# Attention probabilities transposed in 32x32 blocks on VectorE and put in order through DRAM, in place of transposes on TensorE

## The chip, the cores and the metric

The kernel runs on one core of a Trainium2 chip, in one launch. The metric is the time of the execution on the device in microseconds, the median over the runs. Lower is better.

## The reference, cut to what matters

One layer of a graph transformer over 128 graphs of 128 nodes, width 384, eight heads of 48, all in float32:

```python
q = split_heads(x @ wq + bq); k = split_heads(x @ wk + bk); v = split_heads(x @ wv + bv)
scores = einsum('bhqd,bhkd->bhqk', q, k) * dh ** -0.5 + adj[:, None]
attn = softmax(scores, axis=-1)
ctx = einsum('bhij,bhjd->bhid', attn, v)
x1 = rmsnorm(x + ctx @ wo + bo, alpha1, gamma1)
x2 = rmsnorm(x1 + silu(x1 @ w1 + b1) @ w2 + b2, alpha2, gamma2)
out = layernorm(x + x2)
```

The change is about `attn`. The scores come out with the queries on the partitions and the keys along the row. The product with v contracts over the keys, so the keys have to lie on the partitions: every head of every graph needs its 128x128 probabilities transposed.

## The kernel before, in words

Two graphs make a group (`PAIR`); there are 64 groups, 256 tokens each. The matrix products of the layer's weights are made with each operand split in a high and a low part and three products each (`PASSES`), written `passes`, line 443. Weights stay in SBUF for the whole run.

The work is a pipeline over slots, written out by hand for each engine in its own `slot_program(t)`. In slot t the core does: the projections q, k, v of group t; the scores and softmax of group t-1; the context, output product and first norm of group t-2; the feed-forward (`up`, silu, `down`) of group t-3; and the last norm of group t-3 and t-4. There are 68 such slots, 0 to 67. Every engine works through its own list in order, and waits on semaphores where it needs another.

In one slot TensorE (PE) runs, in this order: context of both graphs (L495, L499), scores (L514), output product (L443, `wo_s`), q, k and v (L443), the 108 matmuls of `up` (L443, `w_s`; six pieces m = 0 to 5 of 18 matmuls), the transposes of the probabilities (L470, 16 of them), the transposes of the next group's x (L451 into `ps_work`, 6) and of x1 (L451 into `ps_att`, 6), and the 72 matmuls of `down` (L581).

The two PSUM tiles `ps_work` take turns. Piece m of `up` writes over what piece m-2 left, so it waits for ScalarE's silu of piece m-2:

```python
if m >= 2:
    pe.wait_ge(silu_ready[m - 2], through(g))
```

ScalarE (ACT) makes silu of a piece (L714) from PSUM into `h_raw`, which has two places; VectorE (DVE) then splits it into high and low (L883 and L885). Silu of piece m waits for `h_lo[m - 2]`, the split of piece m-2, because it writes over that place. The transposes of x also write `ps_work`, in two parts: four of them into the tile that piece 4 used, and then two into that of piece 5:

```python
for i, blocks in enumerate(((0, 1), (2,))):
    if live(g - LAG_FF - 1):
        pe.wait_ge(silu_ready[fc // 2 - 2 + i], through(g - LAG_FF - 1))
    ...
    transpose_rows(x_banks[i], x_in, blocks, xT_done[i])
```

Softmax: DVE adds the bias and takes the maximum (L823, L827), ACT takes the exponentials head by head (L660), DVE scales by the inverse sum (L833, L835; `normalise`, two halves of four heads for each graph). PE transposes the probabilities into `ps_att`, and ACT copies them back to `probs` (L649, `probsT_out`); the context of the next slot reads them as the moving operand.

The SP queue issues nearly all DMAs, in order: in a slot the residual x, the bias, the next x, `x_last`, ten small moves of q and k from `qk_flat` to `qk` (L359), the output of an earlier group (L363), and in slots 0 to 3 weights. In slot 3 six loads of w2 (L319) stand last on it; ACT (`weights_hi`, L634) and DVE (`weights_lo`, L802) split them between the silu pieces of that slot: two of them behind silu piece 2, two behind 3, two behind 4.

Of the kernel before, what the change touches and what calls it, by code (L numbers as in the profile page):

```python
# [14 lines left out]
HALF = 64  # L15
TILE = 32
HI, LO = 0, 1

# [8 lines left out]
def build_layer(nc, x, adj, wq, bq, wk, bk, wv, bv, wo, bo, w1, b1, w2, b2,  # L27
# [17 lines left out]
    with ctx:  # L45
# [108 lines left out]
        probsT_done = sems("probsT_done", PAIR)  # L154
        probsT_ready = sems("probsT_ready", PAIR)
        ctx_done = sems("ctx_done", PAIR)
        ctx_hi = sems("ctx_hi", PAIR)
# [43 lines left out]

        probs_words = probs[:].rearrange("p b h n -> p (b h n)")
        h_words = h_raw[:].rearrange("p a n -> p (a n)")
# [70 lines left out]
        def through(g, each=1):  # L274

            return (g + 1) * each

        x_banks = (ps_work[1][:, 0:2 * toks], ps_work[0][:, 0:toks])
        x1_banks = (ps_att[0][:, 0:2 * toks], ps_att[0][:, 2 * toks:3 * toks])
# [5 lines left out]
        def group_rows(ap, g):  # L285

            return ap[g * PAIR:(g + 1) * PAIR].rearrange("b n e -> n b e")

        block = ctx.enter_context(nc.Block())

        @block.sync
        def _(sp):
# [33 lines left out]
            def slot_program(t):  # L326
# [109 lines left out]
        def _(pe):  # L436
# [27 lines left out]
            def transpose_probs(g, b):  # L464
                pe.wait_ge(probs_ready[b], through(g, 2))
                if b == 0 and g == last:
                    for i in range(2):
                        pe.wait_ge(x1T_lo[i], through(g - 1))
                for head in range(HEADS):
                    mm = pe.transpose(ps_att[b][:, head * P:(head + 1) * P], probs[:, b, head, :], ident[:])  # L470
                mm.then_inc(probsT_done[b], 1)

            def transpose_x1(g):
                for b in range(PAIR):
                    pe.wait_ge(x1_ready[b], through(g))

                if g == last - 1:
                    pe.wait_ge(scores_biased[0], through(last))
                else:
                    pe.wait_ge(probsT_ready[0], through(min(g + 1, last)))  # L480
                for i, blocks in enumerate(((0, 1), (2,))):
                    transpose_rows(x1_banks[i], x1[:, g % 2], blocks, x1T_done[i])

            def context(g, b):
                pe.wait_ge(probsT_ready[b], through(g))
                pe.wait_ge(v_ready[b], through(g))
# [5 lines left out]
                for side in range(2):  # L492
                    for pair in range(hp):
                        head = 2 * pair + side
                        pe.matmul(ps_work[b][pair * TILE:(pair + 1) * TILE, 2 * P:3 * P], v_rest[:, g % 2, b, head, :],  # L495
                                  probs[:, b, place(head), :], start=(side == 0), stop=(side == 1))
                for head in range(HEADS):
                    p0, at = head % 4 * TILE, head // 4 * P
                    mm = pe.matmul(ps_work[b][p0:p0 + TILE, at:at + P], v_first[:, g % 2, b, head, :],  # L499
                                   probs[:, b, place(head), :], start=True, stop=True)  # L500
                mm.then_inc(ctx_done[b], 1)

            def scores(g, b):
                if b == 0:
                    pe.wait_ge(qk_moved, through(g, 16 * len(moves)))
                if live(g - 1):
                    pe.wait_ge(probsT_ready[b], through(g - 1))
                if b == 0 and live(g + LAG_SCORES - LAG_FF):
# [76 lines left out]
            def slot_program(t):  # L585
# [43 lines left out]
        def _(act):  # L629
# [17 lines left out]
            def probsT_out(g, b):  # L647
                act.wait_ge(probsT_done[b], through(g))
                act.activation(probs[:, b].rearrange("p h n -> p (h n)"), ps_att[b][:],  # L649
                               ACT.Copy).then_inc(probsT_ready[b], 1)  # L650

# [5 lines left out]
            def exponentials(g, b):  # L657
                act.wait_ge(max_ready[b], through(g))
                for head in range(HEADS):
                    e = act.activation(probs[:, b, head, :], probs[:, b, head, :], ACT.Exp,  # L660
                                       bias=neg_max[:, b, head:head + 1], accum_out=row_sum[:, b, head:head + 1])
# [58 lines left out]
            def slot_program(t):  # L720
# [69 lines left out]
        def _(dve):  # L790
# [27 lines left out]
            def bias_and_max(g, b):  # L818
                dve.wait_ge(scores_done[b], through(g))
                if b == 0:  # L820

                    dve.wait_ge(bias_loaded, through(g, 16))
                dve.tensor_tensor(probs[:, b], ps_att[b][:].rearrange("p (h n) -> p h n", n=P),  # L823
                                  bias[:, b, :].unsqueeze(1).to_broadcast([P, HEADS, P]),
                                  ALU.add).then_inc(scores_biased[b], 1)
                dve.wait_ge(scores_biased[b], through(g))
                dve.tensor_reduce(neg_max[:, b, :], probs[:, b], AX.X, ALU.max,  # L827
                                  negate=True).then_inc(max_ready[b], 1)

            def normalise(g, b, half):  # L830
# [3 lines left out]
                dve.wait_ge(inv_ready[b], through(g, 2) - 1 + half)  # L834
                dve.tensor_tensor(probs[:, b, heads], probs[:, b, heads],  # L835
                                  row_inv[:, b, heads].unsqueeze(2).to_broadcast([P, hp, P]),
                                  ALU.mult).then_inc(probs_ready[b], 1)

            def keys_out(g):
# [76 lines left out]
            def slot_program(t):  # L916
# [93 lines left out]
```

## Time and profile before

| | us |
|---|---|
| median of three runs | 2911.36 (2911.35 to 2911.66) |
| the profiled execution | 2910.08 |
| its span in the trace | 2908.3 |
| TensorE busy | 2882.5 (99%) |
| VectorE busy | 1846.2 (63%) |
| ScalarE busy | 1431.3 (49%) |
| GpSimd busy | 684.3 (24%) |
| DMA, mean rate | 59 GB/s |

The profiled execution is 1.8 us longer than its span, for what lies around the first and the last record. A matmul's row in the timeline begins where it starts and has its modelled end behind the start of the next, so the cost of a run of matmuls is read from one row's start to the start of the next row. "PEld" is the load of the stationary operand, which runs beside the matmuls. `[us <-X]` at the end of a row is the idle time of that engine just before it and who ended it.

### The profile page before, as it was taken

To read this page: it belongs to the slowest core of one execution; us is meant where nothing else is said; L and a number is where in the kernel's file an instruction comes from. 1 tells how busy PE (TensorE), PEld (TensorE's weight loads), DVE (VectorE), ACT (ScalarE), POOL (GpSimd) and SP (SyncE) were. 2 spreads that over 40 slices of the span, in tenths; PEclk is the share of its full clock that TensorE was granted. 3 is DMA by queue.
4 is the path that set the end of the run, shared out by engine and by line. 5 is a ranking of instruction groups with operands and counts; after the bars stand their busy time and mean duration, and the time that the engine had idled before them with its cause. 6 is when DMAs were issued, how large, how long until landed. Compare 5 with 4: busy or idle time off the path is not lost.

```text
span 2908.3 us, 62626 instructions
## 1 busy us (share of the span) xinstructions
PE 2882.5 (99%) x25216; PEld 2841.8 (98%) x25216; DVE 1846.2 (63%) x3621; ACT 1431.3 (49%) x4259; POOL 684.3 (24%) x968
## 2 busy tenths in 40 slices
PE   7999999999999999999999999999999999999998
PEld 7999999999999999999999999999999999999998
DVE  6766666656666566566665666666656666566564
ACT  5544545445445454454544544545445445454452
POOL 0222222221222222212222222222221222222222
PEclk9999999999999999999999999999999999999999
DMA  5211212112112121121221211212112112121110
GB/s 172 76 54 57 65 43 68 56 50 64 54 57 65 41 70 52 53 65 48 63 59 47 66 54 56 64 43 68 56 49 64 54 57 65 41 70 53 52 47 28
DMA packets 155490, 171.93 MB, mean 59 GB/s; under 512 B 18624, under 2 KB 155200, under 8 KB 155200
## 3 DMA queue, kind: packets, MB, share of 16 engines
q1 hardware_dynamic: 151952, 166.92, 19.7%
q8 instruction: 200, 3.28, 0.5%
q10 hardware_dynamic: 3248, 0.99, 0.2%
q14 instruction: 90, 0.74, 0.1%
HBM read 92.35 MB, written 25.17 MB: 40 GB/s over the span
## 4 chain that ended last, share of the span: by engine, by line
PE 97%; DVE 1%; DMA 1%; SPq 1%; ACT 0%; issue 0%; POOL 0%; ACTq 0%; POOLq 0%; DVEq 0%
PE ps_work L443 48%; PE ps_rows L581 27%; PE ps_rows L443 7%; PE ps_att L514 4%; PE ps_att L470 4%; PE ps_work L495 2%; PE ps_work L499 2%; PE ps_att L451 1%; PE ps_work L451 1%; SPq L359 0%; DMA x_in<-in_x 0%; DVE w_s L802 0%; DMA stage<-in_L_gnn_wq 0%; POOL x_in L413 0%; DVE neg_max L827 0%
## 5 line engine op out<-in xcount | busy, mean ns | idle before, releaser
L443 PE MATMUL ps_work<-x1T,w_s 128*128 128x256 f32 x6912 | 821.9, 280 | 1.8 <-ACT h_raw L714 1.8
L443 PEld LDWEIGHTS ps_work<-x1T,w_s 128*128 128x128 f32 x6912 | 819.3, 188 | 2.2 <-ACT h_raw L714 2.2
L581 PE MATMUL ps_rows<-w_s,h 128*128 128x384 f32 x4608 | 815.0, 337 | 0.0
L581 PEld LDWEIGHTS ps_rows<-w_s,h 128*128 128x128 f32 x4608 | 796.2, 188 | 0.0
L714 ACT ACTIVATE h_raw<-ps_work,b_col 128x256 f32<-128x256 f32 x768 | 322.3, 471 | 533.1 <-PE ps_work L443 524.9
L660 ACT ACTIVATE probs<-probs,neg_max 128x128 f32<-128x128 f32 x1024 | 396.4, 391 | 190.3 <-DVE neg_max L827 190.3
L425 POOL TENSOR_TENSOR x<-x,rows 128x768 f32<-128x768 f32 x64 | 117.5, 1836 | 1160.8 <-DVE h L885 1160.8
L689 ACT ACTIVATE squares<-y 128x384 f32<-128x384 f32 x128 | 67.1, 524 | 627.8 <-DVE y L894 627.8
L883 DVE CAST h<-h_raw 128x512 fp32r<-128x512 f32 x384 | 163.8, 427 | 249.0 <-ACT h_raw L714 248.8
L894 DVE TENSOR_TENSOR y<-ps_rows,x 128x384 f32<-128x384 f32 x128 | 71.4, 558 | 385.0 <-PE ps_rows L581 385.0
L885 DVE TENSOR_TENSOR h<-h_raw,h 128x512 fp32r<-128x512 f32 x384 | 265.9, 692 | 13.2
L391 POOL TENSOR_SCALAR mean_sq<-sum_sq 128x1 f32<-128x1 f32 x256 | 53.8, 210 | 816.8 <-ACT squares L678 467.0
L443 PE MATMUL ps_work<-xT,wq_s 128*128 128x256 f32 x1728 | 216.0, 282 | 2.9 <-DVE xT L809 2.9
L443 PE MATMUL ps_rows<-wo_s,ctxT 128*128 128x384 f32 x1152 | 218.1, 343 | 0.5 <-DVE ctxT L814 0.5
L443 PEld LDWEIGHTS ps_work<-xT,wq_s 128*128 128x128 f32 x1728 | 213.6, 190 | 3.5 <-DVE xT L809 3.3
L443 PE MATMUL ps_work<-xT,wk_s 128*128 128x256 f32 x1728 | 213.2, 280 | 0.0
L443 PE MATMUL ps_work<-wv_s,xT 128*128 128x384 f32 x1152 | 211.4, 337 | 1.0 <-DVE qk_flat L845 0.5
L443 PEld LDWEIGHTS ps_work<-xT,wk_s 128*128 128x128 f32 x1728 | 207.4, 188 | 0.0
L443 PEld LDWEIGHTS ps_rows<-wo_s,ctxT 128*128 128x128 f32 x1152 | 197.6, 188 | 8.4 <-issue 0.7
L443 PEld LDWEIGHTS ps_work<-wv_s,xT 128*128 128x128 f32 x1152 | 197.6, 188 | 1.8 <-DVE qk_flat L845 1.1
L660 ACT ACTIVATION_READ_ACCUMULATOR probs<-probs,neg_max 128x1 f32 x1024 | 193.4, 189 | 0.0
L835 DVE TENSOR_TENSOR probs<-probs,row_inv 128x512 f32<-128x512 f32 x256 | 177.9, 695 | 8.7
(75 smaller groups left out, 3439.2 us busy)
## 6 DMA issues: line engine op xcount, KB each, us to landing
x_in<-in_x SPq DMA_DIRECT2D x128, 384.0 KB, 3.2
qk<-qk_flat SPq DMA_DIRECT2D x381, 96.0 KB, 2.3
x_last<-in_x SPq DMA_DIRECT2D x64, 384.0 KB, 3.7
out<-y SPq DMA_DIRECT2D x63, 384.0 KB, 2.7
bias<-in_adj SPq DMA_DIRECT2D x64, 128.0 KB, 2.1
qk<-qk_flat SPq DMA_DIRECT2D x127, 64.0 KB, 2.0
qk<-qk_flat SPq DMA_DIRECT2D x127, 32.0 KB, 2.0
stage<-in_L_gnn_w SPq DMA_DIRECT2D x17, 192.0 KB, 4.0
```

The lines of the kernel that those rows point to most:

```text
L425: pool.tensor_tensor(x1[:, g_ff % 2], x1[:, g_ff % 2], row(B2), ALU.add).then_inc(x1_b2_ready, 1)
L443: mm = pe.matmul(ps_out, stationary(sta), moving(mov), start=(i == 0), stop=(i == n - 1))
L470: mm = pe.transpose(ps_att[b][:, head * P:(head + 1) * P], probs[:, b, head, :], ident[:])
L514: mm = pe.matmul(ps_att[b][:, at:at + P], qk[p0:p0 + dh, Q, c, b * P:(b + 1) * P], qk[p0:p0 + dh, K, c, b * P:(b + 1) * P], start=True, st ...
L581: mm = pe.matmul(ps_rows[b][:, 0:d], h[:, sta, m, b * P:(b + 1) * P], w2_s[:, mov, m, :], start=(m == 0 and i == 0), stop=(m == fc - 1 and ...
L660: e = act.activation(probs[:, b, head, :], probs[:, b, head, :], ACT.Exp, bias=neg_max[:, b, head:head + 1], accum_out=row_sum[:, b, head: ...
L689: act.activation(squares[:], y[:, b, :], ACT.Square, accum_out=sum_sq2[:, b:b + 1]).then_inc(sq2_ready[b], 1)
L714: e = act.activation(h_raw[:, m % 2, j * toks:(j + 1) * toks], ps_work[(m + 1) % 2][:, j * toks:(j + 1) * toks], ACT.Silu, bias=b1_col[:, ...
L835: dve.tensor_tensor(probs[:, b, heads], probs[:, b, heads], row_inv[:, b, heads].unsqueeze(2).to_broadcast([P, hp, P]), ALU.mult).then_inc ...
L883: dve.tensor_copy(hi, h_raw[:, m % 2, :]).then_inc(h_hi[m], 1)
L885: dve.tensor_tensor(h[:, LO, 2 * m:2 * m + 2, :].rearrange("p c n -> p (c n)"), h_raw[:, m % 2, :], hi.bitcast(F32), ALU.subtract).then_in ...
L894: dve.tensor_tensor(y[:, b, :], ps_rows[b][:, 0:d], x1[:, g % 2, b, :], ALU.add).then_inc(res2_ready[b], 1)
```

## The change

The groups 0, 1 and 63 go on as before. For the other 61 (g = 2 to 62), PE's 16 transposes and ACT's two copies are gone. DVE transposes the 128x1024 probabilities of a graph in place, in 32x32 blocks, in one instruction. That leaves block (i, j) in its old place with its inside transposed; the blocks still have to change places. SP stores the whole tile to a DRAM buffer and loads it again, with block (i, j) going to (j, i): one store of 512 KB and four loads of 128 KB for each graph, in runs of 1 KB. For such groups the probabilities are laid out with the key block j outside and the head inside (`by_head`), so that a run of all eight heads is 1 KB long. The steps that read or write `probs` in these groups (L823, L827, L835, L660 and the context's matmuls) see a head as four pieces of 32 numbers, 256 apart.

The waits follow: `context` waits for the four loads (`blocks_loaded`) in place of ACT's copy; `scores` and `transpose_x1` wait for `scores_biased` of the group before, in place of ACT's copy, since nothing but the scores now uses `ps_att` there.

The diff, cut to its core:

```diff
-        probs = sb("probs", [P, PAIR, HEADS, P])
+        probs = sb("probs", [P, PAIR, HEADS * P])
...
+        def by_head(g, b):
+            order = "p (h j r) -> p h j r" if blocks_by_pe(g) else "p (j h r) -> p h j r"
+            return probs[:, b].rearrange(order, h=HEADS, r=TILE)
...
+        def by_dma(g):
+            return min(g, last - 1) - 1
...
+        def blocks_by_pe(g):
+            return g < 2 or g == last
+        probs_dram = nc.dram_tensor("probs_blocks", (PAIR, P, QUARTERS, HEADS * TILE), F32, kind="Internal").ap()
...
+            def move_blocks(g):
+                for b in range(PAIR):
+                    sp.wait_ge(blocks_ready[b], by_dma(g))
+                    if by_dma(g) > 1:
+                        sp.wait_ge(blocks_loaded[b], 16 * QUARTERS * (by_dma(g) - 1))
+                    sp.dma_start(probs_dram[b], probs[:, b].rearrange("p (j c) -> p j c", j=QUARTERS)).then_inc(
+                        blocks_stored[b], 16)
+                for b in range(PAIR):
+                    sp.wait_ge(blocks_stored[b], 16 * by_dma(g))
+                    for j in range(QUARTERS):
+                        sp.dma_start(probs[j * TILE:(j + 1) * TILE, b].rearrange("p (i c) -> p i c", i=QUARTERS),
+                                     probs_dram[b, :, j].rearrange("(i r) c -> r i c", r=TILE)).then_inc(
+                                         blocks_loaded[b], 16)
...
+                if live(t - LAG_SCORES) and not blocks_by_pe(t - LAG_SCORES):
+                    move_blocks(t - LAG_SCORES)
                 for n in loads_due.get((t, 1), ()) if t > 0 else ():
                     load_weights(n)
...
             def context(g, b):
-                pe.wait_ge(probsT_ready[b], through(g))
+                if blocks_by_pe(g):
+                    pe.wait_ge(probsT_ready[b], by_pe(g))
+                else:
+                    pe.wait_ge(blocks_loaded[b], 16 * QUARTERS * by_dma(g))
...
-                                  probs[:, b, place(head), :], start=(side == 0), stop=(side == 1))
+                                  by_head(g, b)[:, place(head)], start=(side == 0), stop=(side == 1))
...
-                if live(g_scores) and g_scores < last:
+                if live(g_scores) and g_scores < last and blocks_by_pe(g_scores):
                     for b in range(PAIR):
                         transpose_probs(g_scores, b)
...
-                if live(g_scores) and g_scores < last:
+                if live(g_scores) and g_scores < last and blocks_by_pe(g_scores):
                     for b in range(PAIR):
                         probsT_out(g_scores, b)
...
+            def transpose_blocks(g, b):
+                dve.wait_ge(probs_ready[b], through(g, 2))
+                dve.transpose(probs[:, b], probs[:, b]).then_inc(blocks_ready[b], 1)
...
                 if live(t):
                     values_out(t, 1)
+                if live(g_scores) and not blocks_by_pe(g_scores):
+                    transpose_blocks(g_scores, 0)
                 if live(g_out):
                     layer_norm(g_out, 1)
...
                     for half in range(2):
                         normalise(g_scores, 1, half)
+                    if not blocks_by_pe(g_scores):
+                        transpose_blocks(g_scores, 1)
                 if live(g_ff):
                     for m in range(fc // 2):
                         split_h(g_ff, m)
```

What that makes of the order of instructions. On PE, from `up` to `down` of a slot in the middle, before:

```order
L443 MATMUL ps_work<-x1T,w_s 128x256 x108
L470 MATMUL ps_att<-ident,probs 128x128 x16
L451 MATMUL ps_work<-ident,x_in 128x128 x6
L451 MATMUL ps_att<-ident,x 128x128 x6
L581 MATMUL ps_rows<-w_s,h 128x384 x72
L495 MATMUL ps_work<-probs,v_rest 32x128 x8
```

and now:

```order
L482 MATMUL ps_work<-x1T,w_s 128x256 x108
L490 MATMUL ps_work<-ident,x_in 128x128 x6
L490 MATMUL ps_att<-ident,x 128x128 x6
L627 MATMUL ps_rows<-w_s,h 128x384 x72
L539 MATMUL ps_work<-probs,v_rest 32x128 x8
```

The transposes of the probabilities no longer stand between `up` and the transposes of x.

On DVE, in the same slot, from the end of `values_out` to the first split of silu's output, before:

```order
L859 TENSOR_TENSOR v_rest<-ps_work,rows 128x4x16 x2
L913 TENSOR_SCALAR y<-y,mean_var,inv_std 128x384
L873 SCALAR_TENSOR_TENSOR x<-x,inv_rms,rows 128x384
L877 TENSOR_TENSOR x<-x,rows 128x384
L833 RECIPROCAL row_inv<-row_sum 128x4
L835 TENSOR_TENSOR probs<-probs,row_inv 128x512
L833 RECIPROCAL row_inv<-row_sum 128x4
L835 TENSOR_TENSOR probs<-probs,row_inv 128x512
L883 CAST h<-h_raw 128x512
L885 TENSOR_TENSOR h<-h_raw,h 128x512
```

and now:

```order
L910 TENSOR_TENSOR v_rest<-ps_work,rows 128x4x16 x2
L888 STREAM_TRANSPOSE probs<-probs 128x1024
L964 TENSOR_SCALAR y<-y,mean_var,inv_std 128x384
L924 SCALAR_TENSOR_TENSOR x<-x,inv_rms,rows 128x384
L928 TENSOR_TENSOR x<-x,rows 128x384
L879 RECIPROCAL row_inv<-row_sum 128x4
L881 TENSOR_TENSOR probs<-probs,row_inv 128x4x4x32
L879 RECIPROCAL row_inv<-row_sum 128x4
L881 TENSOR_TENSOR probs<-probs,row_inv 128x4x4x32
L888 STREAM_TRANSPOSE probs<-probs 128x1024
L934 CAST h<-h_raw 128x512
L936 TENSOR_TENSOR h<-h_raw,h 128x512
```

Two `STREAM_TRANSPOSE` of 128x1024 stand ahead of the first split (CAST and TENSOR_TENSOR of `h`), and the scaling by the inverse sum has its rows in pieces of 32.

On the SP queue, from the last move of q and k (48x2x256) to the next load of x, before:

```order
L359 DMA qk<-qk_flat 48x2x256 x2
L363 DMA out<-y 128x2x384
L310 DMA x_in<-in_x 128x2x384
L341 DMA bias<-in_adj 128x2x128
L300 DMA x_in<-in_x 128x2x384
```

and now:

```order
L396 DMA qk<-qk_flat 48x2x256 x2
L400 DMA out<-y 128x2x384
L349 DMA probs_blocks<-probs 128x1024 x2
L354 DMA probs<-probs_blocks 32x4x256 x8
L333 DMA x_in<-in_x 128x2x384
L378 DMA bias<-in_adj 128x2x128
L323 DMA x_in<-in_x 128x2x384
```

Two stores and eight loads stand between the output and the load of the residual; in slot 3 they stand ahead of the six loads of w2.

## Rows read from the trace of the kernel before

**Rows 1.** Page: the chain that ended last, by engine.

```profile
PE 97%; DVE 1%; DMA 1%; SPq 1%; ACT 0%; issue 0%; POOL 0%; ACTq 0%; POOLq 0%; DVEq 0%
```

**Rows 2.** Waits of TensorE from 180 to 2800 us (us, times, longest).

```profile
PE ps_att L451 <- ACT probs L649: 0.3, 1, 0.3
```

**Rows 3.** Timeline, PE, one slot: start, us, engine, line, out<-in.

```profile
1504.06 0.65 PE L495 MATMUL ps_work<-probs,v_rest 128*32 128x128 f32 x16
...
1505.94 2.06 PE L514 MATMUL ps_att<-qk 48*128 48x128 f32 x32
...
1520.64 12.83 PE L443 MATMUL ps_work<-x1T,w_s 128*128 128x256 f32 x108
...
1533.32 1.91 PE L470 MATMUL ps_att<-ident,probs 128*128 128x128 f32 x16
1535.06 0.82 PE L451 MATMUL ps_work<-ident,x_in 128*128 128x128 f32 x6
...
1536.29 8.92 PE L581 MATMUL ps_rows<-w_s,h 128*128 128x384 f32 x50
...
1548.95 0.65 PE L495 MATMUL ps_work<-probs,v_rest 128*32 128x128 f32 x16
```

**Rows 4.** Timeline, ACT, same slot.

```profile
1522.95 0.84 ACT L714 ACTIVATE h_raw<-ps_work,b_col 128x256 f32<-128x256 f32 x2 [2.14 <-PE ps_work L443]
...
1533.51 0.84 ACT L714 ACTIVATE h_raw<-ps_work,b_col 128x256 f32<-128x256 f32 x2 [1.27 <-PE ps_work L443]
```

**Rows 5.** Timeline, DVE, same slot.

```profile
1525.04 0.70 DVE L885 TENSOR_TENSOR h<-h_raw,h 128x512 fp32r<-128x512 f32 x1
```

**Rows 6.** Groups by form, whole run: xcount, busy us, mean ns.

```profile
L827 DVE TENSOR_REDUCE neg_max<-probs 128x8 f32<-128x1024 f32 x128 | 156.2, 1220 | 4.4
L883 DVE CAST h<-h_raw 128x512 fp32r<-128x512 f32 x384 | 163.8, 427 | 249.0 <-ACT h_raw L714 248.8
L857 DVE TENSOR_TENSOR v_first<-ps_work,rows 128x256 f32<-128x256 f32 x128 | 53.9, 421 | 4.3 <-PE ps_work L443 2.2
```

**Rows 7.** Timeline around 2822 us, slot 64: who released silu and TensorE.

```profile
2821.99 0.69 DVE L885 TENSOR_TENSOR h<-h_raw,h 128x512 fp32r<-128x512 f32 x1
2822.78 0.84 ACT L714 ACTIVATE h_raw<-ps_work,b_col 128x256 f32<-128x256 f32 x2 [4.04 <-DVE h L885]
2823.67 4.50 PE L443 MATMUL ps_work<-x1T,w_s 128*128 128x256 f32 x36 [1.07 <-ACT h_raw L714]
```

**Rows 8.** Timeline, SP queue, same slot as rows 3.

```profile
1518.68 6.98 SPq L359 DMA_DIRECT2D qk<-qk_flat  x10
1525.76 0.54 SPq L363 DMA_DIRECT2D out<-y  x1
1535.95 0.37 SPq L310 DMA_DIRECT2D x_in<-in_x  x1
```

**Rows 9.** Page, DMA issues: KB each, median us to landing.

```profile
out<-y SPq DMA_DIRECT2D x63, 384.0 KB, 2.7
bias<-in_adj SPq DMA_DIRECT2D x64, 128.0 KB, 2.1
stage<-in_L_gnn_w SPq DMA_DIRECT2D x17, 192.0 KB, 4.0
```

**Rows 10.** Timeline, slot 3: up, the six w2 loads, the copies and silu of piece 3.

```profile
84.06 12.83 PE L443 MATMUL ps_work<-x1T,w_s 128*128 128x256 f32 x108
...
88.85 2.99 SPq L319 DMA_DIRECT2D stage<-in_L_gnn_w  x6
...
91.57 1.02 ACT L634 ACTIVATE w_s<-stage 128x384 fp32r<-128x384 f32 x2
92.70 0.84 ACT L714 ACTIVATE h_raw<-ps_work,b_col 128x256 f32<-128x256 f32 x2
```

**Rows 11.** Timeline: TensorE after an early gap; and its clock there (third from the right).

```profile
24.81 2.77 PE L514 MATMUL ps_att<-qk 48*128 48x128 f32 x32 [3.19 <-DMA qk<-qk_flat]
24.80:27.50 2.70, 2.69 (x32) 2.48 (x32) 1.64 (x3) 0.89 (x3) 0.00 (x0) 0.71 0.66 230
```

More of the change, by code:

```diff
@@ L16 @@
 TILE = 32
+QUARTERS = P // TILE
 HI, LO = 0, 1
@@ L155, in build_layer @@
         probsT_ready = sems("probsT_ready", PAIR)
+        blocks_ready = sems("blocks_ready", PAIR)
+        blocks_stored = sems("blocks_stored", PAIR)
+        blocks_loaded = sems("blocks_loaded", PAIR)
         ctx_done = sems("ctx_done", PAIR)
@@ L200, in staged_at @@
             return n if n < places else (n - places) % STAGE_SLOTS
-        probs_words = probs[:].rearrange("p b h n -> p (b h n)")
+        probs_words = probs[:].rearrange("p b n -> p (b n)")
         h_words = h_raw[:].rearrange("p a n -> p (a n)")
@@ L276, in through, with by_pe @@
             return (g + 1) * each
+        def by_head(g, b):
+            order = "p (h j r) -> p h j r" if blocks_by_pe(g) else "p (j h r) -> p h j r"
+            return probs[:, b].rearrange(order, h=HEADS, r=TILE)
+        def by_pe(g):
+            return g + 1 if g < 2 else 3 if g == last else 2
+        def by_dma(g):
+            return min(g, last - 1) - 1
         x_banks = (ps_work[1][:, 0:2 * toks], ps_work[0][:, 0:toks])
@@ L469, in transpose_probs @@
                 for head in range(HEADS):
-                    mm = pe.transpose(ps_att[b][:, head * P:(head + 1) * P], probs[:, b, head, :], ident[:])
+                    mm = pe.transpose(ps_att[b][:, head * P:(head + 1) * P], probs[:, b, head * P:(head + 1) * P], ident[:])
                 mm.then_inc(probsT_done[b], 1)
@@ L475, in transpose_x1 @@
                     pe.wait_ge(x1_ready[b], through(g))
-                if g == last - 1:
-                    pe.wait_ge(scores_biased[0], through(last))
+                if g + 1 > last:
+                    pe.wait_ge(probsT_ready[0], by_pe(last))
+                elif g + 1 < last and blocks_by_pe(g + 1):
+                    pe.wait_ge(probsT_ready[0], by_pe(g + 1))
                 else:
-                    pe.wait_ge(probsT_ready[0], through(min(g + 1, last)))
+                    pe.wait_ge(scores_biased[0], through(g + 1))
                 for i, blocks in enumerate(((0, 1), (2,))):
@@ L499, in context @@
                     mm = pe.matmul(ps_work[b][p0:p0 + TILE, at:at + P], v_first[:, g % 2, b, head, :],
-                                   probs[:, b, place(head), :], start=True, stop=True)
+                                   by_head(g, b)[:, place(head)], start=True, stop=True)
                 mm.then_inc(ctx_done[b], 1)
@@ L505, in scores @@
                     pe.wait_ge(qk_moved, through(g, 16 * len(moves)))
-                if live(g - 1):
-                    pe.wait_ge(probsT_ready[b], through(g - 1))
+                if live(g - 1) and blocks_by_pe(g - 1):
+                    pe.wait_ge(probsT_ready[b], by_pe(g - 1))
+                elif live(g - 1):
+                    pe.wait_ge(scores_biased[b], through(g - 1))
                 if b == 0 and live(g + LAG_SCORES - LAG_FF):
@@ L647, in probsT_out @@
             def probsT_out(g, b):
-                act.wait_ge(probsT_done[b], through(g))
-                act.activation(probs[:, b].rearrange("p h n -> p (h n)"), ps_att[b][:],
-                               ACT.Copy).then_inc(probsT_ready[b], 1)
+                act.wait_ge(probsT_done[b], by_pe(g))
+                act.activation(probs[:, b], ps_att[b][:], ACT.Copy).then_inc(probsT_ready[b], 1)
             def context_hi(g, b):
@@ L659, in exponentials @@
                 for head in range(HEADS):
-                    e = act.activation(probs[:, b, head, :], probs[:, b, head, :], ACT.Exp,
+                    e = act.activation(by_head(g, b)[:, head], by_head(g, b)[:, head], ACT.Exp,
                                        bias=neg_max[:, b, head:head + 1], accum_out=row_sum[:, b, head:head + 1])
@@ L822, in bias_and_max @@
                     dve.wait_ge(bias_loaded, through(g, 16))
-                dve.tensor_tensor(probs[:, b], ps_att[b][:].rearrange("p (h n) -> p h n", n=P),
-                                  bias[:, b, :].unsqueeze(1).to_broadcast([P, HEADS, P]),
+                dve.tensor_tensor(by_head(g, b), ps_att[b][:].rearrange("p (h j r) -> p h j r", j=QUARTERS, r=TILE),
+                                  bias[:, b, :].rearrange("p (j r) -> p j r", r=TILE).unsqueeze(1).to_broadcast(
+                                      [P, HEADS, QUARTERS, TILE]),
                                   ALU.add).then_inc(scores_biased[b], 1)
                 dve.wait_ge(scores_biased[b], through(g))
-                dve.tensor_reduce(neg_max[:, b, :], probs[:, b], AX.X, ALU.max,
+                dve.tensor_reduce(neg_max[:, b, :], by_head(g, b), AX.XY, ALU.max,
                                   negate=True).then_inc(max_ready[b], 1)
@@ L834, in normalise @@
                 dve.wait_ge(inv_ready[b], through(g, 2) - 1 + half)
-                dve.tensor_tensor(probs[:, b, heads], probs[:, b, heads],
-                                  row_inv[:, b, heads].unsqueeze(2).to_broadcast([P, hp, P]),
+                dve.tensor_tensor(by_head(g, b)[:, heads], by_head(g, b)[:, heads],
+                                  row_inv[:, b, heads].unsqueeze(2).unsqueeze(3).to_broadcast(
+                                      [P, hp, QUARTERS, TILE]),
                                   ALU.mult).then_inc(probs_ready[b], 1)
+            def transpose_blocks(g, b):
+                dve.wait_ge(probs_ready[b], through(g, 2))
+                dve.transpose(probs[:, b], probs[:, b]).then_inc(blocks_ready[b], 1)
             def keys_out(g):
```

## The prediction

> **What bounds the kernel now.** I read the chain of waits first. TensorE holds 97% of it [rows 1]. Then its waits: from 180 to 2800 us TensorE waited once, for 0.3 us [rows 2]. So every matmul taken off this engine shortens the kernel, unless a wait opens in its place. The other engines matter only through what TensorE waits for, and TensorE waits for none of them because each is in time; the question is by how much. That is read inside one slot, since all slots from 3 to 62 run alike: from one context to the next is 1548.95 - 1504.06 = 44.89 us [rows 3].
>
> The 16 transposes of the probabilities start at 1533.32 and those of x at 1535.06 [rows 3]: 1.74 us a slot, 0.109 us each.
>
> **What the removed transposes cover.** The transposes of x begin with four that need silu piece 4 and go on with two that need silu piece 5. That silu runs from 1533.51 to 1534.35 [rows 4], and `up` ends just before 1533.32. Now the probabilities' transposes fill this time. Without them the first four start at 1533.32 and are done at 1533.32 + 4 x 0.109 = 1533.76. The other two wait for 1534.35 plus the step from silu to TensorE. In slot 64 that step can be seen: silu ends at 2822.78 + 0.84 = 2823.62, TensorE starts at 2823.67 [rows 7], 0.05 us; I take 0.08, hence 1534.43. New stall: 0.67 us. A slot gains 1.74 - 0.67 = 1.07 us, if nothing else comes late.
>
> **What VectorE gets.** Two transposes of 128x1024 in place stand ahead of the first split of silu's output. No row shows this operation. The nearest in size is the maximum over 128x1024 at 1.22 us [rows 6]. Below it, two CASTs of 128x512 at 0.427 give 0.85 us, for an operation that reads and writes faster. Above it, two passes over the tile give 2.44 us. I take 1.22, since the maximum too goes over 1024 elements once. The Trainium skill, Vector Engine (DVE) Microarchitecture Reference, section 3.8, says that the transpose is pipelined to sustain one element per cycle in each lane; nothing in this trace shows it, and the sum by it would be the one below.
>
> The first split now ends at 1525.04 + 0.70 = 1525.74 [rows 5]. It moves by 2 x 1.22 = 2.44 to 1528.18. Silu piece 2 writes over what it reads. The step from a split to silu is seen in slot 64: the split ends at 2822.68, silu starts at 2822.78 [rows 7], 0.10 us. So silu 2 starts at 1528.28, ends 0.84 later, and TensorE can begin piece 4 at 1529.17. A piece of `up` takes (1533.32 - 1520.64) / 6 = 2.11 us, so piece 4 is due at 1520.64 + 4 x 2.11 = 1529.09 [rows 3]. The stall is 0.08; I take 0.1. In general it is the shift less 2.36 us: **the free room is almost exactly used up**. Piece 5 needs silu 3, which needs the second split, at 1528.18 + 1.2 = 1529.4; silu 3 would be done near 1530.4 and piece 5 is due at 1531.2, so nothing more is lost. Net gain of a slot: 1.07 - 0.1 = **0.97 us**.
>
> **Edits taken at nothing.** DVE's bias, maximum and scaling work in pieces of 32. `v_first` is already written in pieces of 32: 256 elements at 421 ns [rows 6], against 1024 at 1220. The difference is 799 ns for 768 elements, one rate for both shapes. The exponentials on ACT are in pieces too; ACT is idle 2.14 us before silu piece 0 [rows 4]. Without that cover, each 0.1 us of lateness in silu would cost up to 6 us over 60 slots. The context's matmuls read pieces of 32 as the moving operand. They take from 1504.06 to 1505.94 [rows 3], 1.9 us a slot; I take no change since the columns are as many, and the bounds are 0 and that time again. ACT's two copies vanish; nothing waited for them but the transposes of x1, in slot 63. `scores` waits for `scores_biased`, a slot old.
>
> **The way through DRAM.** SP issues the output until 1525.76 + 0.54 = 1526.30 [rows 8], then store 0. Store 1 needs DVE's second transpose, near 1527.1. A 384 KB output lands in 2.7 us and 192 KB of weights in 4.0 [rows 9]; for 512 KB I take 3, bounds 2.1 and 5.3. Store 0 has landed at 1529.3. Eight loads at 0.55 an issue (between 0.37 and 0.70 [rows 8]) are out by 1533.7 and landed 2.1 us later (128 KB, bias [rows 9]), at 1535.8. The context that needs them is due at about 1548. That is 12 us of room, on a path that takes ten, so nothing is lost. The residual x behind them on SP goes out at 1535.95 now [rows 8], later than 1533.7, so it isn't held up.
>
> **Slot 3, once.** The six w2 loads now stand behind this traffic. Before, they were issued from 88.85; the copies of the first two began at 91.57, silu 3 at 92.70 [rows 10]. After: store 0 at 88.85, landed 91.9, eight issues at 0.55 until 96.3; the first w2 load is 7.5 us late. ACT stands in its copies until 91.57 + 7.5 = 99.1. Silu 3 starts at 100.2 and ends at 101.1, where piece 5 is due at 84.06 + 5 x 2.11 = 94.6: TensorE idles 6.5 us. Silu 4 and 5 each follow two copies, 1.95 us apiece, so silu 5 ends at 105.0. Eight transposes later `down` starts at 105.9. It was due 15.65 us after `up` (as in rows 3) less 0.97, at 98.7: 7.2 us lost. After an early gap of 3.19 us the granted clock was 0.71 for 2.7 us [rows 11], between the levels of 1.2 and 2.4 GHz, 0.8 us of work lost. I add 0.8 for that: **8 us**, bounds 5 and 12.
>
> **Slot 63** has no transposes of x. It gains 1.74 and the one wait of 0.3 behind ACT's copy [rows 2], less 0.1: 2.0 us.
>
> **Sum.** 60 x 0.97 = 58.2, plus 2.0, less 8 = 52.2 us. The profiled execution took 2910.08 us, its span 2908.3. 2910.1 - 52.2 = 2857.9. The median of the runs lies 1.3 above the profiled execution: **2859 us**. A measurement of this kernel can tell about 0.2%, 6 us, from no change.
>
> **Rivals.**
> 1. *The transpose on VectorE is slow.* At two passes, 2.44 us each, the shift is 4.88 and piece 4 stalls 4.88 - 2.36 = 2.52 us. A slot loses 2.52 - 1.07 = 1.45 us. With slot 63 (loses 0.45) and slot 3 (8) the time is 2911.4 + 87 + 8.5 = **3007 us**, slower. It decides from 1.66 us a transpose: there the stall is 0.96 and the gains are gone. For it: 4-byte elements move across lanes, and no row shows the rate. Against: every float32 operation of DVE in this trace runs at least at the rate of the maximum. Chance 0.12. Between 1.5 and 1.66 us the time is 2892 to 2911; with other small losses the stretch from 2885 to 2905 gets 0.08.
> 2. *The context's matmuls slow down with pieces of 32.* Doubled, they cost 1.9 us in each of 61 slots: 2859 + 116 = 2975 us. Every other moving operand here is contiguous, so the trace is silent. 0.03.
> 3. *The blocks come late.* Every us beyond the 12 of room costs 60 us; at 14 us more than I take, 2859 + 120 = 2979. It would need landings over three times those of [rows 9]. The Trainium skill, VectorE: DVE Perf Modes, "The three transpose paths", warns that a plain DMA that transposes by strides can be 19 times slower than the hardware's transposing DMA when the destination's innermost stride is large; here that stride is one element and the runs are 1 KB. 0.02.
> 4. *The cover isn't needed*: the transposes of x don't stall, and no `up` piece does. 60 x 1.74 + 2 - 8 = 98 us, **2813 us**. The silu row speaks against it: it ends 0.6 us after the four transposes would. 0.04.
> 5. *Nothing to measure*, the stall near break-even or the gain lost elsewhere: 2911, 0.03.
>
> The same page of the Trainium skill, "Rules for kernel authors", says to transpose 128x128 on TensorE if PSUM will do as destination. It speaks against the change and would give rival 1's sign. The rows say otherwise here: the engine it favours is the one in the chain, and VectorE has room for all but 0.1 us.
>
> **Chances.** The forecast, 2848 to 2885, has 0.68. With the stretch above it (0.08) and rival 4 (0.04) faster has 0.80; same 0.03; slower 0.12 + 0.03 + 0.02 = 0.17. The low end of the range is no stall in `up` (6 us), a slot 3 of 5 us, and a piece of rival 4: 2842. The high end takes in transposes up to 1.6 us: 2908.
>
> **What would show it.** Right: no L470 rows in the middle, slots of 43.9 us, TensorE waiting for silu once at the x transposes for about 0.67 us in 60 slots, and for 0.1 or less in `up`; `STREAM_TRANSPOSE` at 1.2 to 1.3 us; a gap of 6 to 7 us in slot 3; the eight loads landed 10 us ahead of the context. Wrong: a transpose of over 1.6 us, context rows longer than before, or TensorE waiting for `probs` from a DMA.

## The result and the profile after

| | before | after |
|---|---|---|
| median of the runs, us | 2911.5 | 2863.14 (2862.74 to 2863.66, 4 runs) |
| the profiled execution, us | 2910.08 | 2862.81 |
| its span, us | 2908.3 | 2861.0 |

The ratio is 0.9833, with a 95% interval of 0.9821 to 0.9845: 48 us or 1.7% less, where 52 were forecast (2859 us). From the page after, the span, the busy shares and the chain by engine:

```profile
span 2861.0 us, 61404 instructions
...
PE 2799.9 (98%) x24240; PEld 2742.2 (96%) x24240; DVE 1968.0 (69%) x3743; ACT 1326.6 (46%) x4137; POOL 686.1 (24%) x968
...
PE 94%; ACT 2%; DVE 1%; SPq 1%; DMA 1%; issue 0%; POOL 0%; ACTq 0%; POOLq 0%; DVEq 0%
```

TensorE's share of the chain fell from 97% [rows 1] to 94%, and ACT has 2% in it: silu now releases TensorE in every slot. The groups by form (count | busy us, mean ns) give the one price that no row of before had, the last line; the two above it are the steps that now work in pieces of 32:

```profile
L881 DVE TENSOR_TENSOR probs<-probs,row_inv 128x512 f32<-128x512 f32 x256 | 177.9, 695 | 8.7
L873 DVE TENSOR_REDUCE neg_max<-probs 128x8 f32<-128x1024 f32 x128 | 156.2, 1221 | 4.4
...
L888 DVE STREAM_TRANSPOSE probs<-probs 128x1024 f32<-128x1024 f32 x122 | 151.3, 1240 | 2.1
```

The transpose takes 1.24 us for 128x1024, where 1.22 was taken. The maximum in pieces of 32 is at 1221 ns against 1220 [rows 6].

One slot in the timeline, PE, ACT, DVE and SP together, answering to [rows 3, 4, 5, 8]:

```profile
1484.59 0.65 PE L539 MATMUL ps_work<-probs,v_rest 128*32 128x128 f32 x16
...
1501.18 12.94 PE L482 MATMUL ps_work<-x1T,w_s 128*128 128x256 f32 x108
...
1501.98 1.24 DVE L888 STREAM_TRANSPOSE probs<-probs 128x1024 f32<-128x1024 f32 x1
...
1506.36 1.25 DVE L888 STREAM_TRANSPOSE probs<-probs 128x1024 f32<-128x1024 f32 x1
...
1507.95 0.69 DVE L936 TENSOR_TENSOR h<-h_raw,h 128x512 fp32r<-128x512 f32 x1
...
1508.73 0.84 ACT L759 ACTIVATE h_raw<-ps_work,b_col 128x256 f32<-128x256 f32 x2 [2.29 <-DVE h L936]
...
1510.38 3.67 SPq L354 DMA_DIRECT2D probs<-probs_blocks  x8
...
1513.96 0.60 PE L490 MATMUL ps_work<-ident,x_in 128*128 128x128 f32 x4
1514.16 0.84 ACT L759 ACTIVATE h_raw<-ps_work,b_col 128x256 f32<-128x256 f32 x2 [1.28 <-PE ps_work L482]
...
1515.05 0.44 PE L490 MATMUL ps_work<-ident,x_in 128*128 128x128 f32 x2 [0.49 <-ACT h_raw L759]
...
1515.90 12.74 PE L627 MATMUL ps_rows<-w_s,h 128*128 128x384 f32 x72
...
1528.57 0.64 PE L539 MATMUL ps_work<-probs,v_rest 128*32 128x128 f32 x16
```

The next context starts at 1528.57, so a slot is 43.98 us, 0.91 less than the 44.89 of before. `up` runs from 1501.18 to 1513.96, 12.78 us against 12.68: its first split ends at 1508.64, silu piece 2 waits for it and starts at 1508.73. Then four transposes of x start at 1513.96, the two others at 1515.05, behind the silu of 1514.16. From the end of `up` to `down` it is 1.94 us against 2.97 [rows 3]. So a slot gained 1.03 and lost 0.10. The only wait of TensorE that the list of waits has between 180 and 2750 us (us, times, longest):

```profile
PE ps_work L490 <- ACT h_raw L759: 28.6, 58, 0.5
```

The "0.5" is the idle time behind the modelled end of the four transposes; from start to start the row costs 1.09 - 0.44 = 0.65 us.

Slot 3 answers to [rows 10]. The SP queue (two stores, eight loads, then the six w2 loads), then ACT's copies of w2 and TensorE's last piece of `up`, then the window of that piece with TensorE's granted clock third from the right:

```profile
90.78 1.82 SPq L349 DMA_DIRECT2D probs_blocks<-probs  x2
93.76 3.67 SPq L354 DMA_DIRECT2D probs<-probs_blocks  x8
97.47 2.80 SPq L342 DMA_DIRECT2D stage<-in_L_gnn_w  x6
```

```profile
100.88 1.05 ACT L680 ACTIVATE w_s<-stage 128x384 fp32r<-128x384 f32 x2 [6.67 <-DMA stage<-in_L_gnn_w]
...
102.71 4.21 PE L482 MATMUL ps_work<-x1T,w_s 128*128 128x256 f32 x18 [5.99 <-ACT h_raw L759]
```

```profile
102.70:106.70 4.00, 3.99 (x18) 4.00 (x19) 3.93 (x8) 2.33 (x6) 0.00 (x0) 0.50 0.01 2
```

```profile
86.00 10.72 PE L482 MATMUL ps_work<-x1T,w_s 128*128 128x256 f32 x90
...
108.70 12.74 PE L627 MATMUL ps_rows<-w_s,h 128*128 128x384 f32 x72
121.37 0.65 PE L539 MATMUL ps_work<-probs,v_rest 128*32 128x128 f32 x16
```

The w2 loads went out at 97.47 where they had gone out at 88.85; 1.94 us of that is that the slot's `up` itself starts later, at 86.00 where it was 84.06 [rows 10]. ACT waited 6.67 us for them, TensorE 5.99, and then made 18 matmuls at a granted clock of 0.50, which is 1.2 GHz, in 4.0 us in place of 2.1.

The whole difference of the spans can be laid out from the starts of the contexts. Up to the context of slot 4, which began at 112.37 before, the kernel is 121.37 - 112.37 = 9.0 us later. From there to the context of slot 63, 59 slots, it takes 2594.52 us where 2648.70 were taken: 54.2 less. Slot 63 takes 42.60 in place of 44.76: 2.2 less. The rest is alike within 0.1 us. 54.2 + 2.2 - 9.0 = 47.4, against 2908.3 - 2861.0 = 47.3.

The 9.0 us are of two kinds. From the start of `up` in slot 3 to the context of slot 4 it takes 35.37 us where 28.31 were taken, 7.06 more. The other 1.94 were lost ahead of that `up`, and 1.16 of them by 15.07 us (`wk_s` started at 13.91 before), long before any group goes the new way. They don't come from the change: in the eleven traces of this document, the first kernel's among them, TensorE has the same work up to that point, and this `up` starts anywhere between 83.2 and 87.4 us (at 87.3 in experiment 7, which has nothing of the new way). Why the start-up differs so stays open. So a difference of a few us between two medians can be start-up, and the mean time of a slot is given with them below. It is the time from the context of slot 4 to that of slot 63, divided by 59: 44.89 us before and 43.98 after.

### The profile page after: what moved, and what is told of

Its sections match the earlier page's. It is cut to its first block, busy times and chain, and to the rows that moved or that the text cites. A ratio compares the mean times of both kernels' runs of the same rounds, so it can differ in the third digit from the quotient of the medians.

```text
span 2861.0 us, 61404 instructions
## 1 busy us (share of the span) xinstructions
PE 2799.9 (98%) x24240; PEld 2742.2 (96%) x24240; DVE 1968.0 (69%) x3743; ACT 1326.6 (46%) x4137; POOL 686.1 (24%) x968
## 4 chain that ended last, share of the span: by engine, by line
PE 94%; ACT 2%; DVE 1%; SPq 1%; DMA 1%; issue 0%; POOL 0%; ACTq 0%; POOLq 0%; DVEq 0%
PE ps_work L482 48%; PE ps_rows L627 28%; PE ps_rows L482 7%; PE ps_att L560 4%; PE ps_work L539 2%; PE ps_work L543 2%; ACT h_raw L759 2%; PE ps_att L490 1%; PE ps_work L490 1%; SPq L396 1%; DMA x_in<-in_x 0%; DVE w_s L847 0%; DMA stage<-in_L_gnn_wq 0%; POOL x_in L452 0%; DVE neg_max L873 0%
## 5 line engine op out<-in xcount | busy, mean ns | idle before, releaser
L482 PE MATMUL ps_work<-x1T,w_s 128*128 128x256 f32 x6912 | 830.7, 281 | 7.8 <-ACT h_raw L759 7.8
```

The source lines that it names most:

```text
L482: mm = pe.matmul(ps_out, stationary(sta), moving(mov), start=(i == 0), stop=(i == n - 1))
```

## The experiments

The theory to be tested: the change frees 1.74 us of TensorE a slot, and three waits of TensorE give some of it back, each with its own cause. They are silu piece 5 ahead of the last transposes of x (0.65 us), silu piece 2 behind the late split (0.1 us), and the w2 loads of slot 3 (8 to 9 us, once). The rival of each is that the loss comes from something shared (DMA traffic, memory, ACT) and would only move. Every edit is on the kernel after the change unless it says otherwise.

**1. The w2 loads first.**

```diff
+                for n in loads_due.get((t, 1), ()) if t > 0 else ():
+                    load_weights(n)
                 if live(t - LAG_SCORES) and not blocks_by_pe(t - LAG_SCORES):
                     move_blocks(t - LAG_SCORES)
-                for n in loads_due.get((t, 1), ()) if t > 0 else ():
-                    load_weights(n)
```

> The six w2 loads of slot 3 go to the SP queue ahead of the stores and loads of the blocks. My theory: the 6 us gap of TensorE before up piece 5 of slot 3 and the 4.2 us piece at a granted clock of 0.50 behind it come from these loads alone; both go, and slot 3 gets about 8.5 us back: 2863.1 - 8.5 = 2854.6 us. Rival: ACT is late in slot 3 because VectorE's two transposes delay the splits, and the loads are only seen waiting; then the time stays within 2 us of 2863.

Measured 2853.96 us (2853.73 to 2855.89), 9.2 less. Neither the gap nor the slow piece is left in slot 3: `up` takes 12.68 us there. The rival is out.

```profile
84.08 12.83 PE L482 MATMUL ps_work<-x1T,w_s 128*128 128x256 f32 x108
...
111.36 0.64 PE L539 MATMUL ps_work<-probs,v_rest 128*32 128x128 f32 x16
```

From `up` to the next context it is 27.28 us in place of 35.37: the loads cost 8.1 us. The rest isn't theirs: this trace starts `up` 1.92 us earlier, and its later slots take 1.0 us more in all (8.1 + 1.9 - 1.0 = 9.0, the difference of the two spans).

**2. The transposes of x1 between those of x.**

```diff
                 for i, blocks in enumerate(((0, 1), (2,))):
+                    if i == 1 and between is not None:
+                        transpose_x1(between)
...
-                    transpose_x(t + 1)
-                if live(g_attn):
+                    transpose_x(t + 1, g_attn)
+                elif live(g_attn):
                     transpose_x1(g_attn)
```

> The six transposes of x1, which wait for nothing late, go between the four and the two transposes of x. My theory: the wait of 0.65 us before the last two transposes of x is pure lateness of silu piece 5, so six other transposes of 0.65 us fill it, in 60 slots: 60 x 0.65 = 39 us less, 2824 us, and the wait row all but vanishes. Rival: the wait only moves, to the first matmuls of down or to the next slot's context, because silu 5 and the splits behind it set the pace there too: 2850 to 2863 us.

Measured 2824.51 us (2821.91 to 2826.16), 38.6 less; a ratio to the kernel before of 0.9705 [0.9691, 0.972]. The timeline of TensorE at the end of a slot's `up`:

```profile
1534.29 0.60 PE L490 MATMUL ps_work<-ident,x_in 128*128 128x128 f32 x4
1534.73 0.82 PE L490 MATMUL ps_att<-ident,x 128*128 128x128 f32 x6
1535.39 0.44 PE L490 MATMUL ps_work<-ident,x_in 128*128 128x128 f32 x2
1535.58 12.74 PE L629 MATMUL ps_rows<-w_s,h 128*128 128x384 f32 x72
```

All twelve transposes and the start of `down` follow without a wait: 1.29 us in place of 1.94. The time didn't move elsewhere: the mean slot is 43.34 us, 0.64 less.

**3. The second transpose behind the first split.**

```diff
                         normalise(g_scores, 1, half)
-                    if not blocks_by_pe(g_scores):
-                        transpose_blocks(g_scores, 1)
...
                         split_h(g_ff, m)
                         weights_lo(t, m)
+                        if m == 0 and live(g_scores) and not blocks_by_pe(g_scores):
+                            transpose_blocks(g_scores, 1)
```

> VectorE's transpose of the second graph goes behind the first split of silu's output in place of ahead of it. My theory: up takes 12.78 us a slot in place of 12.68 because the first split is late; with the split 1.2 us earlier silu piece 2 is in time and 60 x 0.1 = 6 us are gained: 2857 us. Rival: the 0.1 us comes from traffic (the DMAs now at 105 GB/s, or VectorE and TensorE reading the same memory), and moving the instruction changes nothing: 2863 us.

Measured 2857.71 us (2856.94 to 2858.85), 5.4 less. `up` is back at 12.67 us a slot and the mean slot at 43.86 us, 0.115 less, or 6.8 us over 59 slots; up to slot 4 this trace is 2.8 us later, half of it ahead of `up` in slot 3. The 0.1 us was the late split.

**4. Three transposes of the second graph in place of one.**

```diff
                 dve.wait_ge(probs_ready[b], through(g, 2))
+                if b == 1:
+                    for i in range(2):
+                        dve.transpose(probs[:, b], probs[:, b]).then_inc(blocks_again, 1)
+                        dve.wait_ge(blocks_again, 2 * (by_dma(g) - 1) + i + 1)
```

> VectorE transposes the second graph's tile three times in place (two more of 1.25 us, one after the other). My theory: the room of 2.36 us is used up, so each further us on VectorE ahead of the first split is a us of the slot: 61 x 2.5 = 153 us more, about 3016 us, and slower than the kernel before. Rival: VectorE's lateness is partly absorbed (by the later pieces of up, or by the wait before the transposes of x, which would shrink as up gets longer): under 2960 us.

Measured 3093.20 us (3092.74 to 3093.72), 230 more: 3.77 us a slot for 2.5 us of VectorE. The direction is right, the size isn't. One slot, then the windows behind the gap (clock third from the right):

```profile
1531.17 2.52 DVE L891 STREAM_TRANSPOSE probs<-probs 128x1024 f32<-128x1024 f32 x2
...
1536.11 0.84 ACT L760 ACTIVATE h_raw<-ps_work,b_col 128x256 f32<-128x256 f32 x2 [4.85 <-DVE h L941]
...
1537.00 5.83 PE L483 MATMUL ps_work<-x1T,w_s 128*128 128x256 f32 x36 [2.40 <-ACT h_raw L760]
...
1542.67 0.60 PE L491 MATMUL ps_work<-ident,x_in 128*128 128x128 f32 x4
```

```profile
1537.00:1539.00 2.00, 2.00 (x9) 2.00 (x10) 1.93 (x5) 0.84 (x2) 0.00 (x0) 0.50 0.76 231
1539.00:1541.00 2.00, 2.00 (x15) 2.00 (x14) 0.21 (x1) 0.27 (x1) 0.00 (x0) 0.77 1.00 236
1541.00:1542.60 1.60, 1.60 (x16) 1.60 (x15) 0.97 (x2) 0.57 (x2) 0.00 (x0) 1.00 0.46 98
```

Piece 4 of `up` was due at 1525.99 + 4 x 2.11 = 1534.44 and starts at 1537.00, 2.56 us late. The two pieces left then take 1542.67 - 1537.00 = 5.67 us, where 4.23 is their time at full clock: 1.44 us more. The granted clock is 0.50 for the first 2 us and 0.77 for the next 2. So this wait is paid one and a half times. With the 0.10 us that `up` was late already, 2.56 + 1.44 - 0.10 = 3.90 us, and the slot shown takes 47.86 us, 3.88 more.

**5. A shorter gap.** The same place, with two transposes of half the tile ahead of the one.

```diff
+                        dve.transpose(probs[:, b, 0:4 * P], probs[:, b, 0:4 * P]).then_inc(blocks_again, 1)
```

> Ahead of its transpose of the second graph VectorE transposes the first half of the tile (128x512) twice in place: 2 x 0.71 plus two steps, about 1.47 us more, where the kernel with three whole transposes had 2.5 us more and TensorE idle 2.40 us a slot, with a granted clock of 0.50 for 2 us behind each gap. Theory A, the clock answers to any such wait in up: the gap of about 1.4 us costs about 1.3 us of slow matmuls more, 61 x 2.8 = 170 us, about 3033 us. Theory B, the gap of 1.4 us leaves the clock at full speed, as the one of 0.49 us does: 61 x 1.47 = 90 us, about 2953 us.

Measured 2954.70 us (2953.29 to 2955.63), 91.6 more: 1.50 us a slot for 1.47 of VectorE. Theory B holds. The piece behind the gap, and its window:

```profile
1514.13 4.49 PE L483 MATMUL ps_work<-x1T,w_s 128*128 128x256 f32 x36 [1.33 <-ACT h_raw L760]
```

```profile
1514.10:1516.10 2.00, 1.97 (x16) 1.97 (x17) 1.93 (x5) 0.84 (x2) 0.00 (x0) 1.00 0.72 229
```

TensorE is idle 1.33 us and its clock stays at 1.00. In this `up` a gap of 1.33 us costs itself, one of 2.40 us costs 1.4 us more.

**6. Twice through DRAM**, on top of experiment 1.

```diff
+                for b in range(PAIR):
+                    sp.wait_ge(blocks_loaded[b], 16 * QUARTERS * by_dma(g))
...
+                    sp.dma_start(again_dram[b], probs[:, b].rearrange("p (j c) -> p j c", j=QUARTERS)).then_inc(
+                        again_stored[b], 16)
...
+                        sp.dma_start(probs[rows_j, b].rearrange("p (i c) -> p i c", i=QUARTERS),
+                                     again_dram[b, rows_j]).then_inc(again_loaded[b], 16)
```

> On top of the w2 loads ahead of the blocks (2854.0 us): every block goes to DRAM and back a second time, in the same order, before the context may read it. Traffic of the blocks doubles and the path from the first store to the last landing grows from about 10 to about 20 us. My theory: it had 11 to 12 us of room, so the time stays within 3 us of 2854. Rival: the way through DRAM is already nearly at its limit, or its traffic slows matmuls and other transfers: at least 10 us more, 2864 us or beyond.

Measured 2854.69 us (2852.41 to 2855.58), 0.7 more than experiment 1, within its spread, and the mean slot is 43.97 us against 43.99 there. SP's second trip in a slot, and the context behind it:

```profile
1501.95 3.69 SPq L357 DMA_DIRECT2D probs<-probs_blocks  x8
1506.42 2.53 SPq L364 DMA_DIRECT2D probs_again<-probs  x2
1509.68 4.34 SPq L370 DMA_DIRECT2D probs<-probs_again  x8
```

```profile
1520.08 0.65 PE L554 MATMUL ps_work<-probs,v_rest 128*32 128x128 f32 x16
```

The last load is issued by 1514.02 and, at a median landing of 2.9 us, is there near 1517; the context starts at 1520.08. Even two trips fit, with 3 us left. The mean rate of the DMAs rises from 105 to 150 GB/s, and nothing on TensorE slows.

**7. No transposition at all.**

```diff
-                    pe.wait_ge(blocks_loaded[b], 16 * QUARTERS * by_dma(g))
+                    pe.wait_ge(probs_ready[b], through(g, 2))
...
-                if live(t - LAG_SCORES) and not blocks_by_pe(t - LAG_SCORES):
-                    move_blocks(t - LAG_SCORES)
...
-                    transpose_blocks(g_scores, 0)
...
-                        transpose_blocks(g_scores, 1)
```

> Leaves out the transposition of the probabilities of groups 2 to 62 altogether: no transposes on VectorE, no stores and loads; the context reads the untransposed probabilities. My theory: what VectorE and the DMAs cost here is the 0.1 us a slot of up (6 us) and slot 3 (9 us), so 2848 us; the wait of 0.65 us ahead of the transposes of x stays, since it comes from silu. Rival: the block traffic costs more than its waits show (contention in SBUF or with other DMAs): under 2843 us.

This kernel leaves the transposition out, so what it returns is not the layer's output; only its time is of use. Measured 2847.88 us (2845.38 to 2849.11), 15.3 less: the 9.2 of experiment 1 and the 5.4 of experiment 3 make 14.6. Its mean slot is 43.86 us, the same as in experiment 3, which transposes. The new way of transposing costs nothing beyond the two waits already named. The wait ahead of the transposes of x is there as before.

**8. All three repairs,** the diffs of experiments 1 to 3 together.

> The w2 loads ahead of the blocks, the transposes of x1 between those of x, and VectorE's second transpose behind the first split, together. My theory: the three losses are separate waits of TensorE and add up: 2863.1 - 9.2 - 38.6 - 5.4 = 2810 us. Rival: with one gone another takes its place (down behind the splits, or ACT behind the later transposes of x): over 2818 us.

Measured 2808.20 us (2807.36 to 2809.29). The ratio to the kernel before is 0.9644 [0.9628, 0.966], 103 us less; the three repairs taken singly make 53.2, together 54.9. From 130 us on TensorE waits nowhere in the trace where it didn't in the first kernel (twice, in slot 64). The mean slot is 43.21 us, where 44.89 - 1.74 = 43.15 would be the full gain; experiment 9 shows where the 0.06 are.

**9. The order of experiment 2 in the kernel before,** by the diff of experiment 2 alone: the four of x, the six of x1, the two of x.

> The kernel before the change, with only the order of the last transposes altered: the four of x, the six of x1, the two of x. My theory: the 16 transposes of the probabilities already cover silu piece 5 there, so the new order has no wait to fill: 2911 us, within 2 us. Rival: that order is better in itself, with or without the change: 2905 us or less.

Measured 2916.93 us (2914.75 to 2918.1), a ratio of 1.0018 [1.0009, 1.0028]: there was no wait to fill, as the theory says, but the order costs 5 us, which it didn't foresee. ACT's two copies of the probabilities and the transposes of x and x1:

```profile
1539.88 1.94 ACT L651 ACTIVATE probs<-ps_att 128x1024 f32<-128x1024 f32 x2
...
1540.55 0.60 PE L451 MATMUL ps_work<-ident,x_in 128*128 128x128 f32 x4
1541.05 0.85 PE L451 MATMUL ps_att<-ident,x 128*128 128x128 f32 x6
1541.73 0.38 PE L451 MATMUL ps_work<-ident,x_in 128*128 128x128 f32 x2
```

The mean slot is 44.98 us, 0.09 more, and that is 5.3 us over 59 slots. All of it lies in these rows. From the first of the twelve transposes to `down`, which starts at 1541.87, it is now 1.32 us; in the old order it was 1536.29 - 1535.06 = 1.23 [rows 3]. In experiment 2, where the same order runs without any wait, it is 1.29. So 0.06 us of the 0.09 belong to the order itself, on either side of the change, and it is these 0.06 that experiment 8 doesn't get back. The other 0.03 fit a second effect that isn't shown by a run of its own: the transposes of x1 write `ps_att[0]`, which ACT empties here until 1539.88 + 1.02 = 1540.90, and they start at 1541.05, where four transposes at 0.109 from 1540.55 would have let them start at 1540.99. After the change only the scores, long done, use `ps_att` besides them. The order is worth 39 us after the change because there is a wait to fill; without one it costs a little.

## Why the prediction was right, point by point

- **The bound.** TensorE's waits decided the time throughout: experiments 1 to 3 and 8 take away waits of TensorE and give back what the waits measured.
- **The cover of silu piece 5.** Forecast: 0.67 us a slot of the 1.74 given back. Measured 0.65, and from the end of `up` to `down` 1.03 us gained for 1.07. The eight transposes behind the wait take 1515.90 - 1515.05 = 0.85 us. Shown by experiment 2.
- **The transpose on VectorE.** Taken from the maximum, 1.22 us; measured 1.24. The Trainium skill, Vector Engine (DVE) Microarchitecture Reference, section 3.8, gives one element per cycle in each lane; this trace agrees as far as it can: 1240 ns for 1024 elements is within 2% of the maximum's 1221, and the transposes of 512 elements in experiment 5 take 711 ns, so 512 elements more cost 529 ns, 1.03 ns each. The length of VectorE's cycle stands in no row. Free room 2.36 us, stall 0.08, taken as 0.1; measured 0.10. Shown by experiment 3.
- **Net gain of a slot.** 0.97 forecast; 54.18 / 59 = 0.92 measured. This term of the sum is 3 us too large, most of it in the cover.
- **Slot 3.** 8 us forecast, 8.1 by the trace of experiment 1. That they agree is in part luck, since three parts of the term were off and cancel. Piece 5 of `up` was to be 6.5 us late and was 6.2 (102.71 against 86.00 + 5 x 2.11). Silu 5 behind its copies was to add 0.7 us ahead of `down` and added 0.04, because the slow piece hid it. The clock was to cost 0.8, taken from the row of the early gap at 0.71; the piece behind this gap ran at 0.50 and took 4.0 us in place of 2.1, 1.9 lost.
- **Slot 63.** 2.0 forecast, 2.2 measured.
- **The 4.9 us between the sum and the spans.** The sum of 52.2 us is 4.9 above the 47.3 by which the spans differ: 3.1 in the net gain of a slot, over 59 of them, 1.9 in the start-up ahead of slot 3's `up`, which no term foresaw and which varies as much between traces, and about nothing in the rest.
- **The range.** The ends that the prediction works out, 2842 and 2908 us, are not the ends that it states, 2848 and 2885; the result lies inside both.
- **The way through DRAM.** Nothing forecast, nothing measured (experiments 6 and 7). The room was put at 12 us. The median landings (KB, us):

```profile
probs_blocks<-probs SPq DMA_DIRECT2D x122, 512.0 KB, 3.4
probs<-probs_blocks SPq DMA_DIRECT2D x488, 128.0 KB, 3.1
```

  The loads land in 3.1 us where 2.1 was taken from the bias, the stores in 3.4 where 3 was. Eight issues took 3.67 us where 4.4 was taken. In the slot shown the last load is issued by 1514.05 and landed near 1517.1, 11.4 us ahead of the context. The warning of the Trainium skill (VectorE: DVE Perf Modes, "The three transpose paths") about DMAs that transpose by strides did not bear on loads in runs of 1 KB.
- **The edits at nothing.** Pieces of 32 cost nothing on VectorE (695 and 1221 ns, as before), on ACT (exponentials 392 ns against 391) and in the context's matmuls (276 and 273 ns, as before).
- **Rival 1** was priced too low. At 2.44 us a transpose it was to give 3007 us. Experiment 4 puts the same load on VectorE and gives 3093, because a wait of 2.4 us in each `up` is also followed by a granted clock of 0.50 and 0.77. The break-even at 1.66 us a transpose should stand, since a stall of 0.96 us is shorter than that of experiment 5, which left the clock alone; no run is at that point. One reason given against this rival doesn't hold as written: the scaling takes 695 ns for 512 elements, 1.36 ns each, where the maximum takes 1.19. It holds for what an element more costs, (1220 - 695) / 512 = 1.03 ns.
- The Trainium skill's advice (VectorE: DVE Perf Modes, "Rules for kernel authors") to transpose 128x128 on TensorE if PSUM will do did not hold in this kernel, where TensorE is the bound: leaving it is worth 48 us, and 103 with the three repairs.

## What to carry to other kernels

Work that is taken off the bounding engine may have been the cover for a wait: look at what the next instruction waits for, and put something else there in the same edit (39 us here). When DMAs are put into a queue, read everything that stands behind them in every stage, the start-up too: one order of loads in one slot cost 8 us of 57 (54.2 and 2.2, and 1.0 in slot 3). The room of an engine that isn't the bound is the distance to its next deadline, not its idle share: VectorE was 63% busy and had 2.36 us ahead of silu piece 2.

## What the runs showed of the hardware that was not expected

- A wait of TensorE of 2.40 us inside a dense stretch was followed by a granted clock of 0.50 for 2 us and 0.77 for 2 more, 1.4 us lost each time; behind 5.99 us the clock was 0.50 for 4 us; behind 1.33 us and the 0.65 ahead of the transposes of x it stayed at 1.00.
- The same stretch of the start-up did not always get the same clock. In slot 2 TensorE does 14 transposes with a wait of 0.55 us among them, waits 1.44 us, and goes on with 14 more. Before the change these ran at 0.50 and took 3.2 us; after it, behind the same rows and a wait of 1.43, they ran at 1.00 and took 1.7. So 1.33 us is not shown to be safe everywhere. Rows and windows of before, then of after (clock third from the right):

```profile
63.48 1.97 PE L470 MATMUL ps_att<-ident,probs 128*128 128x128 f32 x8 [1.44 <-DVE probs L835]
63.50:65.20 1.70, 1.70 (x8) 1.70 (x9) 0.86 (x2) 0.00 (x0) 0.00 (x0) 0.50 0.45 115
```

```profile
65.85 1.09 PE L509 MATMUL ps_att<-ident,probs 128*128 128x128 f32 x8 [1.43 <-DVE probs L881]
65.90:66.70 0.80, 0.80 (x8) 0.80 (x9) 0.80 (x2) 0.00 (x0) 0.00 (x0) 1.00 0.38 91
```

- In 32x32 blocks and in place, VectorE's transpose of 4-byte numbers runs at the rate of a plain pass: 1240 ns for 128x1024, against 1221 for the maximum over it.
- Rearranging 1 MB a slot through DRAM, and even 2 MB at a mean of 150 GB/s in the kernel, left TensorE's matmul rows unchanged (276 and 273 ns in the context, 43.97 us a slot).
